# LSTM and mixture kernel on one core: two PSUM columns per gate output in place of three, 48 matmul columns in place of 32

## The reference, cut to what matters

```python
def step(carry, xw_t):                     # LSTM, 1024 times
    a = xw_t + prev_h @ Wh                 # xw = x @ Wx + b;  256 x 1024 weights
    i, f, o = sigmoid of three quarters of a;  g = tanh(a[:, 3 * Hdim:])
    next_c = f * prev_c + i * g
    next_h = o * jnp.tanh(next_c)
x = x + hs                                 # h of every step
x = x + mixture(x, cond)                   # 2 shared experts, 8 routed ones (top 2)
```

## Time and profile before

| | us |
|---|---|
| median of 3 runs | 2023.9 (2023.49 to 2024.84) |
| profiled execution, its own time | 2023.38 |
| its span, first to last instruction | 2021.6 |
| PE busy | 1655.5 (82%) |
| DVE busy | 1619.1 (80%) |
| ACT busy | 806.0 (40%) |
| POOL busy | 135.1 (7%) |
| mean granted TensorE clock | 0.997 of full speed |

### The profile page before, as it was taken

How to read it: one execution, slowest core, us unless ns; L and a number is a source line. 1 busy time by engine, 2 the same in 40 slices (tenths; PEclk the granted TensorE clock), 3 DMA queues, 4 the chain that set the end, 5 groups by cost and what they waited for, 6 DMA issues and landing times. The chain is left out here.

```text
span 2021.6 us, 95636 instructions
## 1 busy us (share of the span) xinstructions
PE 1655.5 (82%) x37356; PEld 1456.2 (72%) x37356; DVE 1619.1 (80%) x14263; ACT 806.0 (40%) x5529; POOL 135.1 (7%) x457
## 2 busy tenths in 40 slices
PE   7888888788888888888888887888888888888888
PEld 6777777777777777777777776777777777777777
DVE  6888788787878878788787877878788787887874
ACT  3554343343433434343343433434334343433432
POOL 0000000000000000000000000000000000000000
PEclk9999999999999999999999999999999999999999
DMA  5000000000000000000000000000000000000000
GB/s 232 3 3 3 3 6 3 6 3 3 6 3 6 3 3 6 3 6 3 6 3 3 6 3 6 3 3 6 3 5 3 4 4 3 6 3 6 3 3 7
DMA packets 7223, 19.85 MB, mean 10 GB/s; under 512 B 1136, under 2 KB 5616, under 8 KB 5872
## 3 DMA queue, kind: packets, MB, share of 16 engines
q1 hardware_dynamic: 6768, 13.73, 1.8%
HBM read 11.63 MB, written 2.10 MB: 7 GB/s over the span
## 5 line engine op out<-in xcount | busy, mean ns | idle before, releaser
L687 PE MATMUL gates<-hh,wh_lo 128*128 128x32 f16 x16384 | 820.7, 194 | 349.1 <-DVE hh L608 346.1
L687 PEld LDWEIGHTS gates<-hh,wh_lo 128*128 128x128 f16 x16384 | 597.9, 98 | 544.5 <-DVE hh L608 541.2
L695 PE MATMUL gates<-hh,wh_hi 128*128 128x32 f16 x16384 | 696.7, 183 | 4.2 <-DVE hh L620 4.2
L578 DVE TENSOR_TENSOR_SCAN gates<-part_fac,gates 128x12 f32<-128x12 f32 x3072 | 395.6, 186 | 262.3 <-PE gates L695 238.7
L330 ACT ACTIVATE gates<-gates 128x4 f32<-128x4 f32 x1024 | 161.8, 158 | 1051.5 <-DVE gates L578 1051.5
L695 PEld LDWEIGHTS gates<-hh,wh_hi 128*128 128x128 f16 x16384 | 572.9, 96 | 6.1 <-DVE hh L620 6.1
L340 ACT ACTIVATE to<-o_sum 128x4 f32<-128x4 f32 x1024 | 212.3, 207 | 116.0 <-DVE o_sum L578 0.8
L605 DVE TENSOR_SCALAR to<-to 128x4 f32<-128x4 f32 x1024 | 175.0, 171 | 71.3
L597 DVE TENSOR_TENSOR_SCAN gates<-gates,addend 128x12 f32<-128x12 f32 x1024 | 194.9, 190 | 0.0
L591 DVE SCALAR_TENSOR_TENSOR addend<-gates,c_now 128x4 f32<-128x4 f32 x1024 | 167.7, 164 | 25.1
L333 ACT ACTIVATE addend<-gates 128x8 f32<-128x8 f32 x1024 | 182.2, 178 | 0.0
(11 more groups left out here) (131 smaller groups left out, 1571.3 us busy)
## 6 DMA issues: line engine op xcount, KB each, us to landing
rw_sb<-rw SPq DMA_DIRECT2D x2, 2048.0 KB, 22.2
sw_sb<-sw SPq DMA_DIRECT2D x3, 1024.0 KB, 13.3
outT<-osb SPq DMA_DIRECT2D x16, 128.0 KB, 2.2
x_sb<-xT SPq DMA_DIRECT2D x1, 1920.0 KB, 9.7
wh_sb<-wh SPq DMA_DIRECT2D x1, 1024.0 KB, 4.7
wx_sb<-wx SPq DMA_DIRECT2D x1, 1024.0 KB, 6.5
x_sb<-xT SPq DMA_DIRECT2D x1, 128.0 KB, 4.8
eye_sb<-eye SPq DMA_DIRECT2D x1, 64.0 KB, 6.0
```

What stands on the lines that cost most here:

```text
L578: return v.tensor_tensor_scan(dst, part_fac[:].rearrange("p c j -> p (c j)"), parts[q], 0.0, ALU.mult, ALU.add)
L687: mm(copies(q, m, n)[:, :, :, 0:1], wh_lo[:, c, (q * KC + m) * P:(q * KC + m + 1) * P], again(hh[:, c, :, 1:2], n), start=(m == 0 and c == ...
L695: last = mm(copies(q, m, n)[:, :, :, 0:2], wh_hi[:, c, (q * KC + m) * P:(q * KC + m + 1) * P], again(hh[:, c, :, :], n), start=False, stop ...
```

## The change

- PARTS is 2. x's part is multiplied by `unit` (by POOL in `stage`, into every other column of `seeds`) and written by DVE into the column to which PE adds `wh_hi` times `h_hi`; the other column gets the zero beside it. All `low` matmuls have start=False; four matmuls at the start write zeros over 384 columns of each gate's bank.
- WIDE is 48: `low` writes 24 copies of 2, `high` of G and O 12 copies of 4. `high` of F and I writes one copy, 4 columns.
- `hh` is laid out (part, batch), where it was (batch, part); `high` writes in that order too.
- `low(F)` stands behind `low(I)` and waits for F's seed; `low(O)` waits for O's seed (semaphore `s_seeded`).
- DVE's order behind L608 is changed; `o_sum` is in PSUM; scans have 8 columns.
- ACT's tanh of F, G, I and O takes its scale from a register, loaded once.
- `split` leaves POOL: ACT makes `x_hi` at step 60, DVE `x_lo` at steps 61 and 63.

```diff
-PARTS = 3
-WIDE = 32
+PARTS = 2
+WIDE = 48
 APART = 16
+BESIDE = 384
...
-        hh = sb("hh", [P, KC, B, 2], F16)
-        h_lo, h_hi = hh[:, :, :, 0], hh[:, :, :, 1]
+        hh = sb("hh", [P, KC, 2, B], F16)
+        h_lo, h_hi = hh[:, :, 0, :], hh[:, :, 1, :]
...
-                g.tensor_copy(seeds[:, q % 2, :, :].rearrange("p s g -> p (s g)"), xw[:, first]).then_inc(s_staged, 1)
+                g.tensor_tensor(seeds[:, q % 2, :, :, 1].rearrange("p s g -> p (s g)"), xw[:, first],
+                                unit.broadcast_to([P, HS * GATES]), ALU.mult).then_inc(s_staged, 1)
...
+            act.wait_ge(s_scale, 5)
+            by_unit = nc.scalar.alloc_register("by_unit")
+            nc.scalar.reg_load(by_unit, to_tanh[0:1, :].bitcast(U32))
...
-                activation(tf, last_of(f_sum), ACT.Tanh, scale=0.5).then_inc(s_tanh, 1)
+                activation(tf, last_of(f_sum), ACT.Tanh, scale=by_unit).then_inc(s_tanh, 1)
...
+            def split_hi(tile):
+
+                activation(x_part[0][:], x_sb[:, :, (tile + 2) * TT:(tile + 3) * TT], ACT.Identity, scale=s_xin).then_inc(s_parts, 1)
...
-                v.tensor_copy(gif_xw, of_gif(seeds[:, piece % 2, at, 0:O * HC]))
+                v.tensor_copy(gi_seed, seeds[:, piece % 2, at, 0:F * HC, :].rearrange("p (q c) j -> p q (c j)", c=HC))
...
                 v.tensor_tensor(h_now, to1[:], tc, ALU.mult).then_inc(s_own, 1)
 
+                v.tensor_copy(parts[F], seeds[:, piece % 2, at, F * HC:O * HC, :].rearrange("p c j -> p (c j)")).then_inc(s_seeded, 1)
+
+                dve.wait_ge(s_own, 2 * s + 2)
+                v.scalar_tensor_tensor(h_lo, h_hi, -LO, by_batch(h_now), ALU.mult, ALU.add).then_inc(s_hlo, 1)
+
                 ins = v.tensor_scalar(c_now[:], cs[:, :, 2], 0.5, None, ALU.mult)
...
-                v.tensor_copy(o_xw, seeds[:, piece % 2, at, O * HC:GATES])
-                dve.wait_ge(s_own, 2 * s + 2)
-                v.scalar_tensor_tensor(h_lo, h_hi, -LO, by_batch(h_now), ALU.mult, ALU.add).then_inc(s_hlo, 1)
+                v.tensor_copy(parts[O], seeds[:, piece % 2, at, O * HC:GATES, :].rearrange("p c j -> p (c j)")).then_inc(s_seeded, 1)
...
-                        mm(copies(q, m, n)[:, :, :, 0:1], wh_lo[:, c, (q * KC + m) * P:(q * KC + m + 1) * P],
-                           again(hh[:, c, :, 1:2], n), start=(m == 0 and c == 0), stop=False, skip_group_check=True)
+                        mm(copies(q, m, n)[:, :, :, 0], wh_lo[:, c, (q * KC + m) * P:(q * KC + m + 1) * P],
+                           hh[:, c, 1:2, :].broadcast_to([P, n, B]), start=False, stop=False, skip_group_check=True)
...
-                        last = mm(copies(q, m, n)[:, :, :, 0:2], wh_hi[:, c, (q * KC + m) * P:(q * KC + m + 1) * P],
-                                  again(hh[:, c, :, :], n), start=False, stop=True, skip_group_check=True)
+                        last = mm(copies(q, m, n).rearrange("p r b j -> p r j b")[:, :, 0:2, :],
+                                  wh_hi[:, c, (q * KC + m) * P:(q * KC + m + 1) * P],
+                                  hh[:, c, :, :].rearrange("p (r j) b -> p r j b", r=1).broadcast_to([P, n, 2, B]),
+                                  start=False, stop=True, skip_group_check=True)
...
-                low(F)
                 low(G)
                 low(I)
+                if s:
+                    pe.wait_ge(s_seeded, 2 * s - 1)
+                elif tile:
+                    pe.wait_ge(s_seeded, 2 * TS - 1)
+                low(F)
 
                 pe.wait_ge(s_hlo, s + 1)
-                high(F).then_inc(s_mul, 1)
-                high(G).then_inc(s_mul, 1)
-                high(I).then_inc(s_mul, 1)
+                high(F, 1).then_inc(s_mul, 1)
+                high(G, WIDE // B // 2).then_inc(s_mul, 1)
+                high(I, 1).then_inc(s_mul, 1)
```

More of the change, by code:

```diff
@@ L147, in cond_resid_kernel @@
         tops, s_wh, s_wx, s_xin = scale[:, 0, :], scale[:, 3, 0:1], scale[:, 3, 1:2], scale[:, 3, 2:3]
-        sc = sb("sc", [P, 6])
-        unit, one_unit, half_lo, s_wh_lo, wh_g, wh_g_lo = (sc[:, j:j + 1] for j in range(6))
+        sc = sb("sc", [P, 7])
+        unit, two_unit, to_tanh, half_lo, s_wh_lo, wh_g, wh_g_lo = (sc[:, j:j + 1] for j in range(7))
         xw_scale = sb("xw_scale", [P, 2])
@@ L379, in _ @@
                 first_tile(s)
+                if s == SPLIT_HI:
+                    split_hi(0)
             take_back(act, s_sum, 5 * TS)
@@ L386, in _ @@
                     mixture(s, xw_at)
+                    if s == SPLIT_HI and it < NT - 1:
+                        split_hi(it)
                 take_back(act, s_sum, 5 * TS)
@@ L434, in _ @@
             dve.wait_ge(s_xwp0, 1)
+            link(v.memset(fac, 1.0))
+            link(v.memset(fac[:, :, 0], 0.0))
             link(v.tensor_copy(hw0[:], acc_lg[:, 0:GATES]))
@@ L471, in _ @@
             dve.wait_ge(s_xwc0, MC + 1)
-            v.tensor_copy(gif_xw, of_gif(xw[:, 0:O * HC]))
-            v.tensor_copy(o_xw, xw[:, O * HC:GATES]).then_inc(s_hhi, 1)
+            for q in range(4):
+                ins = v.tensor_scalar(parts[q].rearrange("p (c j) -> p c j", j=PARTS)[:, :, 1], xw[:, q * HC:(q + 1) * HC], unit, None,
+                                      ALU.mult)
+            ins.then_inc(s_hhi, 1)
             v.memset(hw0[:], 0.0).then_inc(s_hlo, 1)
@@ L653, in first_tile, with split_lo @@
                                            wx_slice(wx_part[0], i, 2 * NW), ALU.mult, ALU.subtract).then_inc(s_lo, 1)
+            def split_lo(k, tile):
+                dve.wait_ge(s_parts, tile + 1)
+                ins = v.scalar_tensor_tensor(x_part[1][:, k, :], x_sb[:, k, (tile + 2) * TT:(tile + 3) * TT], s_xin,
+                                             x_part[0][:, k, :], ALU.mult, ALU.subtract)
+                if k == KC - 1:
+                    ins.then_inc(s_xpart, 1)
             for s in range(TS):
@@ L663, in _ @@
                     mixture(s, ch)
+                    if s in SPLIT_LO and it < NT - 1:
+                        split_lo(SPLIT_LO.index(s), it)
                 round_end()
@@ L676, in copies @@
                 return at[:, :, m * B * PARTS:(m + 1) * B * PARTS].rearrange("p r (b j) -> p r b j", j=PARTS)
-            def again(at, n):
-                return at.rearrange("p b (r j) -> p r b j", r=1).broadcast_to([P, n, B, at.shape[2]])
             def low(q):
@@ L779, in mixture @@
                             last.then_inc(s_xwp, 1)
+            pe.wait_ge(s_link, 1)
+            for q in range(4):
+                mm(gates[:, q * BANK:q * BANK + BESIDE], wx_part[1][:, 0, 0:P], wx_part[1][:, 0, 0:BESIDE], start=True, stop=True)
             pe.wait_ge(s_lw, 32)
@@ L804, in _, with lstm @@
             last.then_inc(s_lg, 1)
-            def lstm(s):
+            def lstm(s, tile):
                 pe.wait_ge(s_hhi, s + 1)
-                low(F)
                 low(G)
                 low(I)
-                pe.wait_ge(s_hlo, s + 1)
-                high(F).then_inc(s_mul, 1)
-                high(G).then_inc(s_mul, 1)
-                high(I).then_inc(s_mul, 1)
+                if s:
[3 more added lines that the diff above has]
+                low(F)
+                pe.wait_ge(s_hlo, s + 1)
+                high(F, 1).then_inc(s_mul, 1)
+                high(G, WIDE // B // 2).then_inc(s_mul, 1)
+                high(I, 1).then_inc(s_mul, 1)
+                if s:
+                    pe.wait_ge(s_seeded, 2 * s)
+                elif tile:
+                    take_back(pe, s_seeded, 2 * TS)
                 low(O)
-                high(O).then_inc(s_mul, 1)
+                high(O, WIDE // B // 2).then_inc(s_mul, 1)
             def first_tile(s):
```

61 lines of the change are left out of this document (22 added, 39 removed).

## The result

Four runs of the changed kernel gave a median of 2261.2 us (2260.68 to 2262.31); four of the kernel before, on the same chip, 2024.37 (2023.49 to 2025.26). The ratio is 1.1171, interval 1.1151 to 1.119: 237 us slower, 6 above the forecast of 2255. The profiled execution has a span of 2258.9 us, at a granted clock of 0.997 as before.

What follows compares the result with a forecast made beforehand. A chain through several engines, with PE's matmuls from first `low` to I's last `high` on it, bounds each step; +234 ns by 1,024 steps is +239.6 us, less 7.5, giving 2255 us, range 2130 to 2340.

Steps and rivals of the forecast that it cites:

- The pace of `low`, +160 ns: Twelve `low` matmuls before the first `high` go from 29.2 to 42.5 ns each: +160 ns per step.
- G wide, +70: G's four `high` matmuls, now wide, go from 25 to 42.5 ns each: +70 ns per step.
- thin I, -12: Thin `high` of F and I keep their pace; I's last has 28 columns fewer to stream: -12 ns per step.
- Scans, -8: DVE scans of 8 columns in place of 12: between 0 and -15 ns, taken as -8 per step.
- O's slack used up, +24: O's wide matmuls delay the O scan, so the cell scan starts later: +20 to +30 ns, taken as +24 per step.
- `split`, -7.5 us: `split` leaving GpSimd ends a slowdown of DVE and a late first `high` once per tile: -7.5 us in all.
- The register, 0: ACT's tanh scaled from a register costs nothing extra; L337 stays at 0.16 us.
- The start, 0: Four 384-column matmuls and a memset at the start lie under the wait for the weights: 0.
- Wide matmuls are free: Rival: `low` was slow from strided `hh` reading; all matmuls go at 25 ns, 1953 us; chance 0.13.
- Only `low` is slow: Rival: pairs inside one instruction merge whatever their order, so only `low` slows, +143 us, 2160 us; chance 0.09.
- A price per instruction: Rival: 29 ns is paid per instruction, not column; wide matmuls stay at 29 and 25 ns, 2000 us; chance 0.04.
- The register costs ACT its 90 ns: Rival: the register scale costs ACT 90 ns; 2345 us with the forecast; no separate chance given.

Runs made afterwards that it cites:

- experiment 1: Changed kernel with each output column's unread copies placed directly behind it, in runs of neighbouring PSUM words, same 48 columns: 1960.38 us, ratio 0.9693 to the kernel before.
- experiment 3: Kernel before with only the new layout of `hh`, PSUM written in the old order: 2021.6 us, ratio 0.9993.
- experiment 4: Kernel before with `high` writing the same four words of each copy in the order 0, 3, 1, 4 instead of 0, 1, 3, 4: 2075.07 us, ratio 1.0252.
- experiment 8: experiment 1 with the early GpSimd add of experiment 5 and WIDE = 52, so runs of 26 words: 1978.61 us, ratio 0.9779 to the kernel before.
- experiment 9: experiment 1 with the early GpSimd add of experiment 5, still 48 columns: 1953.9 us, ratio 0.9656 to the kernel before.
- experiment 11: experiment 9 with `high` of F and I 48 columns wide at all steps: 1959.56 us, ratio 0.9687 to the kernel before.
- experiment 7: Kernel before with only `split` moved from GpSimd to ACT (step 60) and DVE (steps 61 and 63): 2015.88 us, ratio 0.9965.
- experiment 6: Changed kernel with the four tanh taking their scale from SBUF, one value per partition, instead of the register: 2390.26 us, ratio 1.1818 to the kernel before.
- experiment 5: Changed kernel with a one-column GpSimd add right behind the first maximum over partitions: 2254.36 us, ratio 1.1145 to the kernel before.

## Why the prediction was right, step by step

**The pace of `low`, +160 ns: right.** By medians, first `low` to first `high` went from 0.359 to 0.506, +147; the distance behind the first matmul is 39 ns in both kernels, and the twelfth 13 ns show behind the first `high` (29 ns to the next, then 42.5). The reason given, two cycles for each place visited in PSUM, is what experiments 1, 3 and 4 bear out: at full clock 48 columns in runs cost no more than 4 (1), reading is free (3), order alone costs 4 ns per `high` (4). One formula gives the paces at full clock, but for experiment 8: visits to aligned pairs of words x 0.833 + 2.5 ns, at least 25. That is 32 visits 29.2, 48 visits 42.5, 24 visits 25 by the floor. At half clock it gives 64, 96 and 48 cycles, that is 53.3, 80 and 40 ns, and measured are 53 (experiment 4's `high`), 80 and 40 ns. The Trainium skill (PSUM — Partial Sum Buffer, Specifications) has the lines of 8 bytes; the price of one visit is from these rows. Experiment 8 fits it at half clock and lies 2 ns above it at full clock.

**G wide, +70, and thin I, -12: right in size.** Before, F's and I's scans were 0.20 apart; after, the three scans span (0.45 - 0.18) = 0.27, F to G 0.19 on average and G to I 0.09. The forecast had 0.17 and 0.10. It took I's scan as waiting for PE; in fact it stands right behind G's scan on DVE (the tanh of I starts 0.03 after its scan ends, as before). The path moved from PE to DVE over that short piece, and the size came out alike. The 12 ns of the thin ones are 15 when measured in both gates (experiments 9 and 11).

**Scans, -8: right to a few ns.** An 8-column scan takes 0.18 for 0.19; the groups give 177 ns for 186.

**O's slack used up, +24: right.** The O scan and the cell scan are 0.09 apart with no idle time between them (1004.26, 1004.35), as the forecast placed them. The size was a little short: the cell scan starts 0.440 after I's, where the forecast had 0.427.

**All of it:** +234 ns forecast. Measured, with `split`'s 7.1 us taken out of the steps' sum again, (229.9 + 7.1)/1,023 = +232; the median step grew from 1.903 to 2.138, +235. Part by part, in medians: `h_hi` to the first `low` 0.219, then 0.209 (-10; the forecast has no such term); first `low` to I's scan 0.859, then 1.079 (+220, forecast 160 + 70 - 12 = 218); I's scan to the cell scan 0.411, then 0.440 (+29, forecast 24 - 8 = 16); cell scan to the next `h_hi` 0.414, then 0.410 (-4, no term). The large part is forecast to 2 ns; that the whole agrees to 1 is luck, for +13 and -14 cancel.

**`split`, -7.5 us: right,** 7.1 alone (experiment 7). **The register, 0: right,** 158 ns as an immediate (experiment 6); of the bounds 0 and 91 the upper one belongs to an operand in memory. Where a register's value is held, the forecast's reason, no run shows; experiment 6 shows the price. **DVE's order, no wait: right,** the waits show none.

**The start, 0: wrong, +7.6 us.** "GpSimd's stage becomes a multiply" was costed by duration and cover in the running steps, where it is hidden, and the first one was not looked at. The multiply is GpSimd's first two-input operation after the maximum over partitions, and starts 9.5 us later than the copy did; DVE waits 6.28 for it. Experiment 5 takes 6.7 of the 7.6 back (24.69 for 31.39). The traces show what stands there: two configuring instructions of GpSimd at 21.8 us, ahead of L255, 9.0 us before it starts; in the kernel before they come at 36.2, behind the first copies and ahead of L279. That these 9 us are theirs is inferred from the place alone. The forecast gives no order for GpSimd.

**The rivals.** *Wide matmuls are free* fell with experiments 1 and 3: the strided reading it blamed costs nothing, and 48 columns go at 25 ns only where they are written side by side. *Only `low` is slow*, merged pairs whatever their order, fell with experiment 4, and by G's 42.5 ns. *A price per instruction* fell with the 42.5 ns of the same twelve instructions. *The register costs ACT its 90 ns* fell with experiment 6.

## What to carry to other kernels

A matmul's cost depends on where and in what order its columns land in PSUM, so filler columns belong in unbroken runs of words, of even length (experiment 8): here the same 48 columns cost 42.5 or 25 ns. Where a floor hides what a column costs, a stretch of the same kernel at half clock shows it: there 48 columns in runs rose from 25 to 40 ns, the thin `high` from 25 to 28 at most (experiment 1). And where an operation changes its kind on GpSimd, look at its first use, and at what GpSimd ran before it, not at the running loop alone.

## What was not expected of the hardware

- At 52 columns the pace at full clock was 26 to 27.5 ns, where 48 columns in runs gave 25; the count of visits, which fits at half clock, gives 24.2 and 25.8. Cause open.
- The stretches at half clock come and go with how the columns are arranged, not only with how many there are. With 48 columns scattered (the changed kernel) the mean is 0.997 although TensorE waits for `hh` in each step; in runs, with the same columns and thin `high` in F and I, it is 0.986 to 0.988. Nine steps in 64 with wide `high` bring it to 0.995, all of them to 0.997. What about the scattered columns holds the clock up was not tried apart; with them PE is busy 88% of the span, in experiment 9 82%.
- GpSimd's 7.6 to 10.3 us of idle time ahead of its first add or multiply after a maximum over partitions, where a copy started when its input was ready.
- DVE's `h_lo` at 0.60 us beside GpSimd's subtraction and 0.16 without it, at the same step (experiment 7).
